# Moving one of eight one-hot products from VectorE to GpSimd, and two reorderings around it, in a graph kernel on Trainium2

## The reference

```python
def _L0_gnn_ref(x, edge_index, edge_attr, W1, b1, gamma, beta, W2, b2):
    row, col = edge_index
    h = concatenate([x[row], x[col], edge_attr]) @ W1 + b1
    mu = mean(h, axis=0); var = mean((h - mu) ** 2, axis=0)
    h = relu((h - mu) * rsqrt(var + BN_EPS) * gamma + beta)
    msgs = h @ W2 + b2
    sums = segment_sum(msgs, row); counts = segment_sum(ones, row)
    return sums / (counts + 1.0)[:, None] + x

def _L1_gnn_ref(x, W0, b0, W1, b1, W2, b2, edge_index):
    # self loops are added; norm = dinv[src] * dinv[dst]
    conv = lambda h, W, b: segment_sum((h @ W)[src] * norm[:, None], dst) + b
    h = relu(conv(x, W0, b0)); h = relu(conv(h, W1, b1))
    return conv(h, W2, b2)

x = layernorm(x + _L0_gnn_ref(x, ...)); x = layernorm(x + _L1_gnn_ref(x, ...))
```

## Time and profile before

| | us |
|---|---|
| median of 3 runs (lowest, highest) | 3799.39 (3799.33, 3801.58) |
| the profiled execution's own time | 3800.09 |
| its span in the trace | 3798.3 |
| PE busy / PEld busy | 3624.6 (95%) / 2585.7 |
| DVE busy | 2510.9 (66%) |
| ACT busy / POOL busy | 1500.2 (39%) / 962.0 (25%) |

### The profile page before, as it was taken

One profiled execution on the slowest core, in us unless ns is written; L12 is line 12 of the kernel. 1 busy time (PEld: TensorE's weight loads), 2 busy tenths in 40 slices (PEclk: granted clock), 3 DMA queues, 4 the chain that ended last, 5 costly groups with the idle time before them and its releaser, 6 DMA issues.

```text
span 3798.3 us, 104239 instructions
## 1 busy us (share of the span) xinstructions
PE 3624.6 (95%) x40722; PEld 2585.7 (68%) x40943; DVE 2510.9 (66%) x3683; ACT 1500.2 (39%) x3822; POOL 962.0 (25%) x916
## 2 busy tenths in 40 slices
PE   4699999999998899999999999999999999999999
PEld 4588888888888677777777777774444544454444
DVE  6999999999995798898889888973111111111112
ACT  5355555455554466666666666662000000000000
POOL 3000000000000566676767667710000000000000
PEclk8899999999999899999999999999999999999999
DMA  7122322332234455555555555535666566656664
GB/s 246 53 88 87 101 87 85 97 91 87 85 103 148 136 156 157 157 155 156 158 156 154 159 157 156 153 134 182 197 195 200 187 199 196 200 183 211 205 208 133
DMA packets 428707, 569.35 MB, mean 150 GB/s; under 512 B 193778, under 2 KB 353452, under 8 KB 421708
## 3 DMA queue, kind: packets, MB, share of 16 engines
q1 hardware_dynamic: 396908, 510.29, 43.2%
q0 software_dynamic: 25088, 51.43, 5.0%
q10 hardware_dynamic: 6624, 6.42, 0.5%
HBM read 458.48 MB, written 109.53 MB: 150 GB/s over the span
## 4 chain that ended last, share of the span: by engine, by line
PE 92%; DVE 4%; ACT 1%; issue 1%; SPq 1%; DMA 1%; POOL 0%; ACTq 0%; DVEq 0%; POOLq 0%
PE py L1674 31%; PE ph L1364 11%; PE pY L861 11%; PE pSum L1383 10%; PE pbk L922 8%; PE ph L1367 7%; PE pA L848 3%; PE ph L1359 3%; PE pX L853 2%; PE pS L852 1%; PE pbk L899 1%; PE pbk L898 1%; ACT x L1030 1%; DVE prod_raw L1152 1%; PE pg L1660 1%
## 5 line engine op out<-in xcount | busy, mean ns | idle before, releaser
L1312 POOL DMA_INDIRECT q<-pq_dram,chosen x784 | 846.6, 1080 | 385.4 <-issue 198.5
L1674 PE MATMUL py<-ring_raw,p 128*128 128x512 bf16 (+1 forms) x3822 | 785.5, 368 | 4.7 <-DVE g L1792 2.8
L1364 PE MATMUL ph<-p,prod_raw 128*128 (+1 forms) x7056 | 683.2, 219 | 18.6 <-DVE prod_raw L1480 11.9
L1674 PEld LDWEIGHTS py<-ring_raw,p 128*128 128x128 bf16 x3822 | 362.6, 98 | 419.2 <-issue 4.4
L1364 PEld LDWEIGHTS ph<-p,prod_raw 128*128 128x128 bf16 x7056 | 492.6, 98 | 117.3 <-issue 0.7
L1428 ACT ACTIVATE x<-ph 128x512 bf16<-128x512 f32 x588 | 351.4, 598 | 454.2 <-PE ph L1367 320.7
L1367 PE MATMUL ph<-q,prod_raw 128*128 128x128 bf16 x4704 | 519.4, 219 | 0.0
L861 PE MATMUL pY<-p,ring_raw 128*128 128x128 bf16 x7203 | 501.7, 219 | 0.8 <-POOL ring_raw L793 0.4
L1383 PE MATMUL pSum<-x,ring_raw 128*128 128x384 bf16 x2401 | 498.8, 327 | 0.3 <-DVE x L1537 0.3
L1532 DVE SCALAR_TENSOR_TENSOR ring_raw<-ph,x 128x512 f32<-128x512 f32 x588 | 404.2, 687 | 121.2 <-ACT x L1428 121.2
L1850 DVE TENSOR_TENSOR yt<-py,dinv_row 128x512 f32<-128x512 f32 (+1 forms) x39 | 25.8, 661 | 684.1 <-PE py L1674 684.1
(11 more groups left out here) (338 smaller groups left out, 4407.9 us busy)
## 6 DMA issues: line engine op xcount, KB each, us to landing
ring_raw<-at_dram SPq DMA_DIRECT2D x252, 896.0 KB, 4.8
at_dram<-ring_raw SPq DMA_DIRECT2D x49, 1568.0 KB, 5.6
prod_raw<-lrow_dram SPq DMA_DIRECT2D x147, 384.0 KB
prod_raw<-lrow_dram SPq DMA_DIRECT2D x196, 256.0 KB
prod_raw<-lrow_dram SPq DMA_DIRECT2D x49, 416.0 KB
q<-pq_dram,chosen POOLq DMA_INDIRECT x784
arow_dram<-x SPq DMA_DIRECT2D x294, 36.8 KB
x<-arow_dram SPq DMA_DIRECT2D x147, 54.0 KB
```

Source lines behind the costliest of these rows:

```text
L1312: nc.gpsimd.indirect_dma_start(q_rows[i][:, k, :], None, pq_rows, bass.IndirectOffsetOnAxis(ap=chosen[u][:, i, k:k + 1], axis=0)).then_inc ...
L1364: last = nc.tensor.matmul(bank[:, k * P:(k + 1) * P], T[q][:, 0, at:at + P], p_b[:, :, m3, :].rearrange("p a d -> p (a d)"), start=False, ...
L1674: last = nc.tensor.matmul(py[par][:, 0:w], g3[c % 2][:, 7 * i + m, k, :], ring[i][:, 0:w // P, m, :], start=at == m == k == 0, stop=at == ...
```

## The change

There are three edits. The names in the diff are those of the code above; lines of the changed kernel are shifted by 5 to 27 against those of the profile.

1. **The eighth product.** DVE forms products 0 to 6; POOL forms product 7 in one operation of 128×1666 bf16, after it has waited for `prod_used` and `hot_ready`. `prod_ready` now counts two a step. DVE waits for both before it overwrites `hot_p`.
2. **The base counts** of PE (and the turning of the cells) are issued behind the first of the 13 groups instead of ahead of all, and ACT takes them behind the first evacuation.
3. **The moments.** P itself is now the weights of one float32 matmul a block, and the moving side is 131 columns: P scaled by the in-degree, and the three columns of `mom`. The diagonal of the 128×128 result is the weighted sum of squares; the last three columns are the weighted sums, which an additional matmul turns. ACT scales P block by block, 49 operations of 128×128 and seven small copies, in place of seven squares of 128×896.

```diff
@@ sp_1, step
-                            put(sp, S["prod_ready"], s)
+                            put(sp, S["prod_ready"], s * 2)
@@ pool_1, step
+                        if bkt:
+                            if not (isinstance(s, int) and s == 0):
+                                put(pool, S["prod_used"], s)
+                            put(pool, S["hot_ready"], s + 1)
+                            last_field = rec[par][:, 9, :].rearrange("p (g u) -> p g u", u=2).unsqueeze(2)
+                            nc.gpsimd.tensor_tensor(prod[:, :, 7, :, :], hot_p, last_field.to_broadcast([P, TG, B, 2]), ALU.mult).then_inc(S["prod_ready"], 1)
                         if a_:
@@ pe_1, both (the body of bases is the removed head of step, unchanged)
+                                y_group(s, par, g)
+                            if g == 0:
+                                bases(s, m, par, bkt, h_)
@@ pe_1, step
                         if bkt:
-                            pe.wait_ge(S["prod_ready"], s + 1)
+                            pe.wait_ge(S["prod_ready"], s * 2 + 2)
@@ dve_1, step
+                            if not (isinstance(s, int) and s == 0):
+                                dve.wait_ge(S["prod_ready"], s * 2)
                             V.tensor_tensor(hot_p, iota_blk[:].unsqueeze(1).to_broadcast(dims), pairs.to_broadcast(dims), ALU.is_equal).then_inc(S["hot_ready"], 1)
...
-                            for f in range(4, 8):
+                            for f in range(4, 7):
                                 last = product(f)
@@ pe_2
-                            nc.tensor.matmul(pSum[0][0:3, 0:D], mom[:, 7 * i + j, :], pf[:, 7 * i + j, :], start=i == j == 0, stop=i == j == 6)
-                            last = nc.tensor.matmul(pSum[1][0:3, 0:D], mom[:, 7 * i + j, :], psq[i % 2][:, j, :], start=i == j == 0, stop=i == j == 6)
+                            last = nc.tensor.matmul(pSum[0][:, 0:D + 3], pf[:, 7 * i + j, :], psq[i % 2][:, j, :], start=i == j == 0, stop=i == j == 6)
...
                     pe.wait_ge(S["weighed"], 2)
+                    nc.tensor.matmul(pSum[1][0:3, 0:D], p_sums, ident_f[:], start=True, stop=True).then_inc(S["p_turned"], 1)
+                    pe.wait_ge(S["weighed"], 3)
+                    nc.tensor.matmul(st[:, D:2 * D], ones_f[:], own, start=False, stop=False)
+                    pe.wait_ge(S["weighed"], 4)
@@ act_2
+                    act.wait_ge(S["moments_in"], 1)
...
-                        nc.scalar.activation(psq[i % 2][:], pf[:, 7 * i:7 * i + 7, :], ACT.Square).then_inc(S["squared"], 1)
+                        for j in range(7):
+                            nc.scalar.activation(psq[i % 2][:, j, 0:D], pf[:, 7 * i + j, :], ACT.Copy, scale=mom[:, 7 * i + j, 0:1])
+                        nc.scalar.activation(psq[i % 2][:, :, D:D + 3], mom[:, 7 * i:7 * i + 7, :], ACT.Copy).then_inc(S["squared"], 1)
@@ dve_2
-                    for u in range(2):
-                        link(V.tensor_tensor(xs[0:3, u * D:(u + 1) * D], cf[0:3, u * D:(u + 1) * D], pSum[u][0:3, 0:D], ALU.mult))
-                    link(V.tensor_tensor(xs[0:3, 2 * D:3 * D], cf[0:3, D:2 * D], pSum[0][0:3, 0:D], ALU.mult))
+                    V.tensor_copy(p_sums, pSum[0][:, D:D + 3]).then_inc(S["weighed"], 1)
+                    V.tensor_tensor(own, pSum[0][:, 0:D], ident_f[:], ALU.mult).then_inc(S["weighed"], 1)
+                    dve.wait_ge(S["p_turned"], 1)
+                    link(V.tensor_tensor(xs[0:3, 0:D], cf[0:3, 0:D], pSum[1][0:3, 0:D], ALU.mult))
+                    link(V.tensor_tensor(xs[0:3, 2 * D:3 * D], cf[0:3, D:2 * D], pSum[1][0:3, 0:D], ALU.mult))
```

More of the change, by code:

```diff
@@ L863, in y_group, with bases @@
                             last.then_inc(S["y_ready"], 1)
[L865 to L886, removed]
-                            last.then_inc(S["m_used"], 1)
-                    def step(s, m, par, bkt, h_, a_, y_, st_):
-                        moments(s, par, y_, st_)
+                    def bases(s, m, par, bkt, h_):
                         if bkt:
@@ L908, in step, with both, moments @@
                             last.then_inc(S["turned"], 1)
+                    def both(s, m, par, half, bkt, h_, a_, y_):
+                        if a_:
+                            pe.wait_ge(S["hsd_ready"], (s - 2) * 2 + (half + 1))
+                            if half == 0 and not (isinstance(s, int) and s < 3):
+                                pe.wait_ge(S["t_read"], s - 2)
+                        groups = neighbours(s, par, half) if a_ else range(*HALVES[half])
+                        for g in groups:
+                            if y_:
+                                if g == 0:
+                                    pe.wait_ge(S["a_final"], s - 2)
+                                    if not (isinstance(s, int) and s < 4):
+                                        pe.wait_ge(S["y_kept"], s - 3)
+                                y_group(s, par, g)
+                            if g == 0:
+                                bases(s, m, par, bkt, h_)
+                    def moments(s, par, y_, st_):
+                        if st_:
+                            pe.wait_ge(S["y_kept"], s - 3)
+                            last = nc.tensor.matmul(pM[:, 0:2 * D + 7], qp[par], ym[par], start=False, stop=False)
+                        if isinstance(s, int) and s == B + 3:
+                            last = nc.tensor.matmul(pM[:], onesb[:], zerob[:, 0:2 * D].unsqueeze(1).to_broadcast([P, 2, 2 * D]), start=False, stop=True)
+                        if st_:
+                            last.then_inc(S["m_used"], 1)
+                    def step(s, m, par, bkt, h_, a_, y_, st_):
+                        moments(s, par, y_, st_)
                         if isinstance(s, int) and s == 1:
@@ L973, in act_1, with bases, evacuate @@
                             nc.scalar.activation(q3st[(g - 1) % 4][:, 0:w, 1, :], rq[u][:, 0:w, :], ACT.Copy).then_inc(S["mid"], 1)
-                    def evacuate(s, m, par):
+                    def bases(s, m, par, bkt, h_):
+                        if bkt:
+                            act.wait_ge(S["base_ready"], s + 1)
+                            nc.scalar.activation(base_2[:].rearrange("p h k u -> p (h k) u"), pbk[:, BASE:BASE + 2 * B].unsqueeze(2).to_broadcast([P, 2 * B, 2]), ACT.Copy).then_inc(S["based"], 1)
+                        if h_:
+                            act.wait_ge(S["turned"], s)
+                            if not (isinstance(s, int) and s < 3):
+                                act.wait_ge(rows_out[1 - par], 128 * (m - (1 - par)))
+                            nc.scalar.activation(rows_t[1 - par][0:2 * BW, :, :].rearrange("p j s -> p (j s)"), ptr[0:2 * BW, 0:4 * P], ACT.Copy).then_inc(S["rows_ready"], 1)
+                    def evacuate(s, m, par, bkt, h_):
                         c, u = s - 2, par
@@ L1231, in build @@
                 mom = sb("mom", [P, B, 3]); xs = sb("xs", [4, 3 * D])
-                psq = [x1_free[:, u * 7 * D:(u + 1) * 7 * D].rearrange("p (j d) -> p j d", d=D) for u in range(2)]
+                psq = [x1_free[:, u * 7 * (D + 3):(u + 1) * 7 * (D + 3)].rearrange("p (j d) -> p j d", d=D + 3) for u in range(2)]
                 s_raw = sb("s_raw", [P, D]); dinv_rows = sb("dinv_rows", [P, D])
@@ L1235, in build @@
                 nb = [sb(f"nb{u}", [P, D], BF16) for u in range(3)]
+                own, p_sums = bt[0][:], bt[1][:, 0:3]
                 ph = [ps(f"ph{u}", [P, 512]) for u in range(4)]
```

21 lines of the change are left out of this document (8 added, 13 removed).

## The result

| | before | after |
|---|---|---|
| median, us | 3799.55 (4 executions) | 3878.84 (3 executions, 3877.76 to 3878.85) |
| profiled execution, us | 3800.09 | 3877.76 |

The ratio is 1.0206, with a 95% interval of 1.0189 to 1.0223: the changed kernel is 79 us slower. (One more execution of it took 4379.84 us at a mean granted clock of 0.872, where the others had 0.986; it is left out.)

The account below looks back on a forecast made before the run. PE and DVE were both taken as full in stage one's loop, with DVE alone setting the new period. Stage one +90.0 us (+84.3, +6.2, -0.5) and moments -5.4 gave +85, so 3885 us, range 3866 to 3919.

Parts of the forecast that it names:

- DVE is the bound of the step and loses POOL's whole operation: Stage-one loop: DVE stands still 3.0 us a step beside POOL's product, is spared 0.94, and sets the period alone.
- The bound of 2.84: Low bound of DVE's loss per step, in us, from the line with a loss of 0.89 us for 512 elements.
- the case of 1.25 to 2.8 us: Rival: DVE's loss per step lies in this span, so the kernel is slower by less than 75 us; chance 0.03.
- the forecast's own: The main case: DVE loses 2.84 to 3.6 us a step, which gives 3874 to 3919 us; chance 0.82.
- The bound of 3.6: High bound of DVE's loss per step, in us: 1666 elements at 2.0 ns plus 0.2 us of start.
- The line through 128 and 512 elements: DVE's losses beside POOL's operations, 0.24 and 0.93 us, give 1.8 ns an element and 3.0 us for 1666.
- The period: Stage-one loop: 22.20 to 24.07 us a step, +84.3 us over 45 steps; DVE's added wait ahead of `hot_p` costs nothing.
- The first three steps: Steps 0 to 2 of stage one: each gets 3.0 - 0.94 = 2.06 us, together +6.2 us.
- Base counts, 0: Moving PE's base counts behind the first group is worth nothing in the new period, as PE has slack.
- The moments, -5.4: Moments after the loop: 5.8 us sooner with ACT as the bound, less +0.4 of tail; bounds 0 and -7.
- the *hidden* product: Rival: POOL's operation costs DVE nothing, PE sets the period at 21.6 us, 3764 us in all; chance 0.08.
- The clock: Rival: PE's clock falls in its new waits; held 5 us or more a step, 3930 us or more; chance 0.02.

Follow-up runs that it names:

- no_product: The changed kernel with edit 1 taken back, so DVE forms all eight products: 3785.58 us, ratio to before 0.9967.
- product_alone: The kernel before with edit 1 alone (POOL forms the eighth product): 3883.58 us, ratio to before 1.022, one execution.
- two_on_pool: The changed kernel with POOL forming products 6 and 7 and DVE the other six: 3966.94 us, one execution.
- act_part: Against no_product, ACT scales 22 of product 7's 34 columns, DVE the rest: 4093.32 and 4102.16 us, beside 4129.35 and 4133.7 for the kernel before.

## Why the prediction was right

It forecast 3885 us, and 3878.84 were measured. The mechanism was the one it named. The sum was helped a little by luck: it put the loss, the first steps and the end of the loop too high and one gap of 4 us at nothing. By its steps:

- **DVE is the bound of the step and loses POOL's whole operation.** Shown: one long product a step, the loss in proportion to what POOL reads, none with a memset. The term was mis-sized by little: 2.79 us in place of 3.0. The bound of 2.84 was just missed, so that the loss lies in the case of 1.25 to 2.8 us, which had a chance of 0.03, and not in the forecast's own, which had 0.82; the time fell into the range all the same, and would have without the 4 us of the gap below (some 3875 us), since the range reached down to 3866. The bound of 3.6 from the four operations of the earlier trace rows was far off, and so was the estimate of 3.66 us from the Trainium skill's "GPSIMD Engine Reference", section "3.1 Elementwise — side-by-side cycle accounting". The line through 128 and 512 elements was a good guide over a threefold distance: the rate in bf16 is 1.7 ns an element, where it had 1.8.
- **The period.** Forecast 24.07, measured 23.97: 22.03 (DVE's work by no_product) - 0.94 + 2.79 leaves 0.09 us, which is a gap that now stands ahead of `hot_p`, where the prediction put the added wait at nothing. Key and `hot_p` in the loop of the kernel before, 0.03 us between the end of the one and the start of the other:

```profile
603.34 0.24 DVE L1157 SCALAR_TENSOR_TENSOR key<-q,iota_c 128x34 bf16<-128x34 bf16 x1
603.61 1.03 DVE L1161 TENSOR_TENSOR q<-iota_blk,key 128x1666 bf16<-128x1666 bf16 x1
```

In the changed kernel's loop it is 0.14 us (618.83 + 0.24 to 619.21). But in step 3, which is written out and has the same wait, it is still 0.03 (as in steps 1, 2, 4, 5 and 48):

```profile
163.46 0.25 DVE L1174 SCALAR_TENSOR_TENSOR key<-q,iota_c 128x34 bf16<-128x34 bf16 x1
163.74 1.03 DVE L1180 TENSOR_TENSOR q<-iota_blk,key 128x1666 bf16<-128x1666 bf16 x1
```

So the 0.1 us is not the price of a satisfied wait. It belongs to the form that the wait has in the hardware loop, where the listing shows a register operation more (L1179) and the count, `s * 2`, depends on the turn; which part of that takes the time is open. Over the 45 steps, 42 of them in the hardware loop, the mean is the 0.09 us above, and the sum is +79.7 us in place of +84.3.

- **The first three steps.** Forecast +6.2, measured 164.81 - 161.03 = +3.8. Two idle spells of DVE took part of it: 0.66 us ahead of step 3 is gone, and in step 1 DVE waited 6.56 us for L932 where it had been 7.60 for L922, since that took 7.53 us in place of 8.57. The first products also started 0.16 us sooner (93.98 for 94.14), and each step lost 1.85 us and not 2.06.
- **The end of the loop.** -0.5 forecast, -1.1 measured (60.10 us from the last step's first product to `deg_all`, 61.19 before).
- **Base counts, 0.** Right beside edit 1 (4.7 us for edits 2 and 3 together, which the moments account for). Alone they are worth 7.7 us.
- **PE's waits.** 0.87 us ahead of the base counts and 1.35 ahead of L932, released by the two operations that were named; forecast 0.8 and 1.7. (The sum for `orank` writes 15.98 where its row has 615.98; its result of 13.6 us is right.)
- **The moments, -5.4.** Measured -4.7. ACT's batch takes the 2.2 us. PE needs 1.84 us for a batch at the upper clock where 1.55 were forecast, which costs nothing, since ACT is the bound either way. Up to DVE's reading it is 5.3 us less where 5.8 were forecast, and the longer tail (copy, turning, handovers) costs more: from the reading to DVE's `prod_raw<-prod_raw,pid` 13.58 us (1336.89 to 1350.47) for 12.75 (1259.97 to 1272.72), +0.8 where I had +0.4.

The measured parts sum to 79.7 + 3.8 - 1.1 - 4.7 = 77.7 us, and the spans differ by 77.6. Of the rivals, the *hidden* product was real as a mechanism (21.5 us a step, 3759 us) but came only with an operation on POOL that reads nothing. The clock did not matter: it was granted at 1.00 in this stretch. product_alone shows 0.97 there, and two_on_pool 0.95 with PE busy 265.7 of 300 us; both kept DVE as the bound and came out where DVE's period puts them. That a lower clock could not bind is thus seen for these sizes alone. The prediction's sum for this rival was off: with 5 us a step at the lower level PE would have 21.6 + 2.5 = 24.1 us of work, even with DVE's 24.07, and the +1 us a step of its 3930 us needs 7 us.

## What to carry to other kernels

Before work is moved from a full DVE to POOL, compare what POOL's operation takes from DVE with what it spares: here two inputs cost 1.7 ns an element and spared 0.57 (0.94 us over 1666), so neither share that was run paid. A short operation of POOL that is there already tells the rate, if two like operations of DVE are found of which one runs beside it. In this kernel ACT took such work without holding DVE up; there the issue interval of small operations (0.227 us) set how many fit between its own.

## What the runs showed that I had not expected

- The added wait of DVE, which is satisfied long before, costs 0.1 us in each step of the hardware loop and nothing in the steps that are written out.
- ACT's 34 small scaled copies a step cost the kernel 62 us against no_product; 22 of them shorten the loop by 17 us. In these two runs ACT's group was longer than PE's 1.1 us in the one (1.16) and shorter in the other (0.93).
- The addition of the identity, 0.42 us on an idle machine, is worth 11.8 us of the whole (3785.58 to 3773.81).
- On two chips both kernels took some 300 us more. In act_part's traces it lies in stage two, with 20% less moved, while the loop kept its times.
